# Attention in a mixture-of-experts layer: one 2048 wide exponential per key tile, and the last PV and Z matmuls of a pair issued ahead of the next pair's scores

## The reference

```python
def _L0_attn_ref(x, Wq, Wk, Wv):          # x: (4, 4096, 1024), 16 heads of 64
    q = (x @ Wq.T).reshape(N, S, H, hd).transpose(0, 2, 1, 3)
    k = (x @ Wk.T).reshape(N, S, H, hd).transpose(0, 2, 1, 3)
    v = (x @ Wv.T).reshape(N, S, H, hd).transpose(0, 2, 1, 3)
    energy = jnp.einsum('nhqd,nhkd->nhqk', q, k)
    attn = jax.nn.softmax(energy / jnp.sqrt(jnp.float32(hd)), axis=3)
    out = jnp.einsum('nhql,nhld->nhqd', attn, v)
    return out.transpose(0, 2, 1, 3).reshape(N, S, D)

def _L0_ffn_ref(tokens, router_w, router_b, expert_w):
...
    probs = jax.nn.softmax(logits, axis=-1)
    top_p, top_i = jax.lax.top_k(probs, TOP_K)
...
    for e in range(E):
        out = out + x @ expert_w[e] * gate[:, e:e + 1]
...
x = _layernorm(x + _L0_attn_ref(x, L0_attn_Wq, L0_attn_Wk, L0_attn_Wv), axis=-1)
x = _layernorm(x + _L0_ffn_ref(x, L0_ffn_router_w, L0_ffn_router_b, L0_ffn_expert_w), axis=-1)
```

## Time and profile before

| | us |
|---|---|
| median of 2 runs | 2903.71 (2902.87 to 2904.54) |
| the profiled execution, its time | 2902.06 |
| its span on the slowest core | 2900.5 (all cores: 2887.2 to 2900.5) |
| PE busy | 2337.3 (81% of the span) |
| ACT busy | 1113.9 (38%) |
| DVE busy | 719.2 (25%) |

### The profile page before, as it was taken

One profiled execution on the slowest core, in us unless ns is written; L12 is line 12 of the kernel. 1 busy time (PEld: TensorE's weight loads), 2 busy tenths in 40 slices (PEclk: granted clock), 3 DMA queues, 4 the chain that ended last, 5 costly groups with the idle time before them and its releaser, 6 DMA issues.

```text
span 2900.5 us, 31993 instructions; the slowest of 8 cores (2887.2 to 2900.5 us)
## 1 busy us (share of the span) xinstructions
PE 2337.3 (81%) x12032; PEld 896.7 (31%) x12032; DVE 719.2 (25%) x1555; ACT 1113.9 (38%) x1153; POOL 59.7 (2%) x80
## 2 busy tenths in 40 slices
PE   6996998898888888888886343999994434899995
PEld 2442322222222222222222111444441111344442
DVE  2332200000000000000002443333336344233336
ACT  0000288888888888888884100000000010000000
POOL 1000100000000000000000000000000000000000
PEclk9998999999999999999998666999997666999998
DMA  6755799950000000000002001122213000222121
GB/s 89 99 76 87 88 111 112 112 74 1 1 1 1 1 1 1 1 1 1 1 1 80 22 15 49 68 74 72 87 59 137 15 22 0 87 87 81 65 87 58
DMA packets 48017, 146.90 MB, mean 51 GB/s; under 512 B 2752, under 2 KB 23264, under 8 KB 46848
## 3 DMA queue, kind: packets, MB, share of 16 engines
q0 software_dynamic: 43264, 128.09, 24.0%
q1 hardware_dynamic: 4608, 16.78, 1.6%
HBM read 197.32 MB, written 41.94 MB: 82 GB/s over the span
## 4 chain that ended last, share of the span: by engine, by line
PE 62%; ACT 14%; DVE 10%; issue 9%; DMA 4%; DVEq 1%; ACTq 0%; POOL 0%; SPq 0%; POOLq 0%
PE s_PS L703 31%; PE s_PS L389 10%; ACT s_RC L450 9%; PE s_PS L288 6%; PE s_PS L225 5%; PE s_PS L301 4%; PE s_PS L246 4%; ACT s_RC L447 3%; DMA s_RC<-xfm 2%; DVE s_RC L526 2%; PE s_PS L313 1%; DMA s_RC<-xqf 1%; DMA s_RB<-ewb 1%; DVE s_RA L717 1%; DVE s_QO L363 1%
## 5 line engine op out<-in xcount | busy, mean ns | idle before, releaser
L703 PE MATMUL s_PS<-s_RB,s_QO 128*128 128x512 bf16 x4096 | 931.8, 391 | 137.2 <-DVE s_gates L659 67.4
L389 PE MATMUL s_PS<-s_QO,s_RA 64*128 64x512 bf16 x2048 | 571.8, 386 | 92.7 <-ACT s_RC L450 84.2
L447 ACT ACTIVATE s_RC<-s_PS,s_cb 128x1024 bf16<-128x1024 f32 x512 | 570.7, 1115 | 151.7 <-PE s_PS L389 151.7
L703 PEld LDWEIGHTS s_PS<-s_RB,s_QO 128*128 128x128 bf16 x4096 | 406.9, 100 | 658.0 <-issue 208.5
L450 ACT ACTIVATE s_RC<-s_PS,s_cb 128x1024 bf16<-128x1024 f32 x512 | 567.1, 1108 | 0.2 <-PE s_PS L389 0.2
L288 PE MATMUL s_PS<-s_RC,s_RB 128*64 128x512 bf16 x2048 | 329.6, 401 | 39.6 <-DVE s_RC L365 39.6
L761 ACT ACTIVATE s_tE<-s_tB 128x1 f32<-128x1 f32 x16 | 3.2, 203 | 880.6 <-DVE s_tB L753 880.6
L301 PE MATMUL s_PS<-s_RC,s_ozb 128*64 128x512 bf16 x2048 | 303.5, 380 | 0.9 <-ACT s_RC L450 0.9
L363 DVE CAST s_QO<-s_PS 128x1024 bf16<-128x1024 f32 x16 | 19.6, 1225 | 1106.6 <-PE s_PS L288 1106.6
L389 PEld LDWEIGHTS s_PS<-s_QO,s_RA 64*128 64x128 bf16 x2048 | 117.3, 94 | 508.2 <-issue 508.1
L720 DVE SCALAR_TENSOR_TENSOR s_RB<-s_PS,s_gates,s_RA 128x1024 f32<-128x1024 f32 x128 | 164.3, 1283 | 275.3 <-PE s_PS L703 275.3
(11 more groups left out here) (76 smaller groups left out, 643.5 us busy)
## 6 DMA issues: line engine op xcount, KB each, us to landing
s_RB<-ewb POOLq DMA_DIRECT2D x32, 2048.0 KB, 9.6
ewb<-ew POOLq DMA_DIRECT2D x16, 2048.0 KB, 169.1
s_RC<-xfm POOLq DMA_DIRECT2D x16, 1024.0 KB, 11.7
s_RC<-xtm SPq DMA_DIRECT2D x16, 512.0 KB, 3.6
y<-s_RC SPq DMA_DIRECT2D x16, 512.0 KB, 2.6
s_RC<-xqf POOLq DMA_DIRECT2D x4, 1024.0 KB, 18.0
s_RC<-wkT POOLq DMA_DIRECT2D x1, 2048.0 KB, 17.8
s_QO<-wvT POOLq DMA_DIRECT2D x1, 2048.0 KB, 27.0
```

The lines of the kernel that those rows point to most:

```text
L389: ins = t.matmul(PS[:, head * 1024 + qc * 512: head * 1024 + (qc + 1) * 512], RA[rows, c * SQ + kc * 128: c * SQ + (kc + 1) * 128], QO[row ...
L447: sc.activation(P[:, 0:1024], PS[:, 0:1024], AF.Exp, bias=cb3[:, :], scale=0.125).then_inc(sE, 1)
L703: ins = t.matmul(PS[:, pb + jh * 512: pb + (jh + 1) * 512], QO[:, dc * TOK + t_i * 128: dc * TOK + (t_i + 1) * 128], wbuf(par)[:, dc * 102 ...
```

## The change

The two exponentials of a step become one over all 2048 columns, which waits for all four score matmuls and raises sE once. The scores wait once, for the whole exponential of the step before, ahead of all four matmuls. The helpers `emit_zl` and `emit_pvl_fve` are gone: the last PV, the last three Z and DVE's two copies follow right behind the last step of the pair, PV first. `emit_ftz` stays behind the scores of step 2.

```diff
--- before.py
+++ after.py
@@ -331,43 +331,6 @@
         cvE.v += 1
         fvz_cnt[p_prev] = cvE.v
 
-    pvl_exp_need = {}
-
-    def emit_zl(p_prev):
-        cc = p_prev % NPAIR
-
-        def ftZl(t, cc=cc, exp_need=pvl_exp_need[p_prev]):
-            t.wait_ge(sE, exp_need)
-            for kcp in (NKT - 3, NKT - 2, NKT - 1):
-                ins = emit_z(t, cc, kcp, False, kcp == NKT - 1)
-            ins.then_inc(tV, 1)
-        q("tensor", ftZl)
-        ctV.v += 1
-        for kcp in (NKT - 3, NKT - 2, NKT - 1):
-            z_cnt[(p_prev, kcp)] = ctV.v
-
-    def emit_pvl_fve(p_prev):
-        cc = p_prev % NPAIR
-
-        def ftPVl(t, cc=cc, exp_need=pvl_exp_need[p_prev]):
-            t.wait_ge(sE, exp_need)
-            emit_pv(t, cc, NKT - 1, False, True).then_inc(tV, 1)
-        q("tensor", ftPVl)
-        ctV.v += 1
-        pv_cnt[(p_prev, NKT - 1)] = ctV.v
-        pvz_done = ctV.v
-        qc0p = (p_prev // NPAIR) * 1024
-
-        def fve(v, cc=cc, qc0=qc0p, pvz_done=pvz_done):
-            v.wait_ge(tV, pvz_done)
-            v.tensor_copy(QO[:, cc * TOK + qc0: cc * TOK + qc0 + 1024],
-                          PS[:, 2048:3072])
-            ins = v.tensor_copy(zs[:, :], PS[:, 3072:4096])
-            ins.then_inc(vE, 1)
-        q("vector", fve)
-        cvE.v += 1
-        fve_cnt[p_prev] = cvE.v
-
     for h in range(2):
         for c in range(NPAIR):
             p = h * NPAIR + c
@@ -382,8 +345,8 @@
                     if fw > 0:
                         t.wait_ge(vE, fw)
                         t.wait_ge(gC, consts_done)
+                    t.wait_ge(sE, exp_need)
                     for head in range(2):
-                        t.wait_ge(sE, max(0, exp_need - 1 + head))
                         rows = slice(head * 64, (head + 1) * 64)
                         for qc in range(2):
                             ins = t.matmul(
@@ -400,13 +363,8 @@
                 ctS.v += 2
                 s_done = ctS.v
 
-                if p > 0:
-                    if kc == 0:
-                        emit_zl(p - 1)
-                    elif kc == 1:
-                        emit_pvl_fve(p - 1)
-                    elif kc == 2:
-                        emit_ftz(p - 1)
+                if kc == 2 and p > 0:
+                    emit_ftz(p - 1)
 
                 if kc > 0:
                     kcp = kc - 1
@@ -443,19 +401,39 @@
                     if pv_need > 0:
                         sc.wait_ge(tV, pv_need)
                     P = pbuf(kc % 4)
-                    sc.wait_ge(tS, s_done - 1)
-                    sc.activation(P[:, 0:1024], PS[:, 0:1024], AF.Exp,
-                                  bias=cb3[:, :], scale=0.125).then_inc(sE, 1)
                     sc.wait_ge(tS, s_done)
-                    sc.activation(P[:, 1024:2048], PS[:, 1024:2048], AF.Exp,
+                    sc.activation(P[:, 0:2048], PS[:, 0:2048], AF.Exp,
                                   bias=cb3[:, :], scale=0.125).then_inc(sE, 1)
                 q("scalar", fse)
-                csE.v += 2
-
-            pvl_exp_need[p] = csE.v
-
-    emit_zl(2 * NPAIR - 1)
-    emit_pvl_fve(2 * NPAIR - 1)
+                csE.v += 1
+
+            def ftPVl(t, c=c, exp_need=csE.v):
+                t.wait_ge(sE, exp_need)
+                emit_pv(t, c, NKT - 1, False, True).then_inc(tV, 1)
+            q("tensor", ftPVl)
+            ctV.v += 1
+            pv_cnt[(p, NKT - 1)] = ctV.v
+
+            def ftZl(t, c=c):
+                for kcp in (NKT - 3, NKT - 2, NKT - 1):
+                    ins = emit_z(t, c, kcp, False, kcp == NKT - 1)
+                ins.then_inc(tV, 1)
+            q("tensor", ftZl)
+            ctV.v += 1
+            for kcp in (NKT - 3, NKT - 2, NKT - 1):
+                z_cnt[(p, kcp)] = ctV.v
+            pvz_done = ctV.v
+
+            def fve(v, c=c, qc0=qc0, pvz_done=pvz_done):
+                v.wait_ge(tV, pvz_done)
+                v.tensor_copy(QO[:, c * TOK + qc0: c * TOK + qc0 + 1024],
+                              PS[:, 2048:3072])
+                ins = v.tensor_copy(zs[:, :], PS[:, 3072:4096])
+                ins.then_inc(vE, 1)
+            q("vector", fve)
+            cvE.v += 1
+            fve_cnt[p] = cvE.v
+
     emit_ftz(2 * NPAIR - 1)
 
     p2_ve = cvE.v
```

## The result

The changed kernel is slower: 1.1006 of the time before, 95% interval 1.0991 to 1.102. The forecast was 3224 us and slower, range 3183 to 3400. The median of its 11 runs is 3241.66 us (3192.54 to 3328.88), that of before 2903.34. Some executions in any set have one half of the chip at a lower clock and are longer; the ratios leave them out, and so 1.1006 times the 2902 us of before, about 3194 us, is the figure to hold against the working.

The account below looks back on a forecast made before the run. It took ACT and PE, waiting for each other in a ring, to bound the attention stage. Steps 1479.7, passages 46.5 and start 6 made 1532.2 against 1212.2 us, +320.0, so 3224 us; range 3183 to 3400.

Parts of the forecast that it names:

- The chain: Attention steps: scores and exponential never overlap, so every link is paid; 2.89 us a step against 2.235, 1479.7 us in all.
- The slope from L623: Wide exponential: 0.80 ns per element, from L623's 307 ns for 16 elements to L447's 1115 ns, giving 1.94 us.
- The cover: Inside a step: PV and Z, 0.45 + 0.60 us, lie hidden under the exponential of 1.95 us.
- The passage: Between pairs of the attention stage: 3.1 us each, 15 times, 46.5 us; bounds 28 and 65 us.
- scores held back: At a passage: next pair's first scores queue behind PV and twelve Z, starting 1.87 us later than before.
- two slow scores: At a passage: PE idles over 2 us, the clock falls, four scores take 1.04 us, 0.38 more, in two steps.
- the push: At a passage: the transposes of L313 with PV push scores 3 back by 0.45 us.
- The start: First pair of the stage: the clock may take longer to rise; 6 us taken, between 0 and 11.
- The sum: Whole attention stage: 1479.7 + 46.5 + 6 = 1532.2 us against 1212.2, so +320.0 us.
- The clock: PE's clock in the stage: 0.95 or more expected inside a pair, although PE is busy only 60%.
- the likeliest case: The forecast's own case, about 3224 us with the clock kept up inside pairs; chance 0.74.
- this rival: Clock falls in the stage: mostly low, about 3407 us, chance 0.10; partly low, 3260 to 3400 us, chance 0.12.

Follow-up runs that it names:

- e3: Kernel before with both 1024 exponentials kept, but all four score matmuls wait for the second one; ratio 1.1183 to before, lowest 3240.2 us.
- e7: Changed kernel with the four score matmuls of each step issued twice; 3407.6 us at the lowest.
- e6: Changed kernel with the Z matmuls of each step issued twice; 3201.0 us at the lowest.
- e1: Kernel before with one 2048 wide exponential and one wait, passage between pairs left as before; ratio 1.1001 to before, lowest 3186.7 us.
- e2: Changed kernel with the two exponentials and their waits put back, leaving only the new passage order; lowest 2911.4 us against 2898.9 for the kernel before.
- e5: Changed kernel without the Z matmuls of steps 4 to 31; 3405.9 us, a single run.
- e4: Kernel before with Z put between the score matmuls of head 0 and head 1 from step 4 on; ratio 1.0062 to before.
- e8: Kernel before with a step's two halves taken by queries instead of heads; ratio 0.964 to before, lowest 2797.7 us.
- e11: e8 plus Z between the two score halves from step 4 on and the change's passage order; no ratio, lowest 2779.6 us against 2901.1 before.

## Why the prediction was right

- *The chain.* "The two never overlap, so a step is a closed chain, and every link is paid": shown by e3 and e7. Expected 2.89 us a step, measured 2.84. The links: 0.15 (said 0.14), scores 0.61 (0.685 said, from 0.66 and 0.71; the term most off, 0.075 x 512 = 38 us), 0.11, exponential 1.967 (1.95 said, 9 us the other way). The 0.66 is from a passage and the 0.71 from the start of the stage; inside a pair four scores in a row take 0.61. The slope from L623, 0.80 ns an element, was a little low: from 1115 to 1967 ns it is 0.83. The Trainium skill, "ScalarE: Activation LUTs", section What ACT_TABLE_LOAD costs, states 0.833 ns per element, and the trace agrees, (1967 - 1115) / 1024 = 0.832; its 1.99 us for the whole instruction is 0.02 over the measured one.
- *The cover.* PV and Z cost nothing under the exponential: shown by e6, where twice the Z matmuls leave the step at 2.84.
- *The passage.* 3.1 us said, 3.1 measured as the mean of fifteen, 3.34 at the one shown, with the same parts: scores held back (1.87), no stall for DVE, two slow scores, and transposes that push step 3. The exact agreement is part luck: the push, said to be 0.45 us, varies, and the passages lie between 2.5 and 3.34. What the order as such is worth the sum does not say, since it never priced the old order with one exponential: by e1 the new order is 2 us slower in the stage, and by e2, with two exponentials, 12 us.
- *The start.* 6 us said. The clock rose after three steps of 3.26 us, which is 1.3 us.
- *The sum.* +320 said, +289.8 in the stage. Steps account for 26 of the 30 us too many (0.05 x 512), the start for 5, the passages for nothing (46.5 said, 46.4 measured); the 1 left is within the rounding of the step (0.005 x 512).
- *The clock.* It held, as the likeliest case had it, and at the lower level a step is 3.26 us (3.24 said). e5 shows that the 0.22 given to this rival was not idle: without Z it falls. The Trainium skill, "TensorE: Matmul & The Clock Gate", section A second HAM failure mode: psum-queue depth-cycling, warns that short idle times between groups of matmuls can make the clock swing between its levels. The changed kernel has such an idle time of 1.24 us in every step and did not follow it (1.00 inside a pair); e5 came nearer to it, mostly at the lower level (0.54).

## What to carry to other kernels

One wide instruction in place of two saves a fixed cost, here 0.25 us of 2.22 by the durations and 0.10 us of a step by e3, but where two engines share a buffer by halves the halves are the double buffering (one half is filled while the other is read); merging them turns a step from about the longer of two engines' times into a chain of both, hand-overs included. Before widening an instruction, ask who could start on the first half. And choose the halves by what runs side by side on the producer: the same scores split by queries instead of heads gave 3.6%.

## What the runs showed of the hardware

- Taking matmuls away made the changed kernel 212 us slower by way of the clock (e5, 0.54), and a PE without a gap stayed at 0.50 for over 100 us (e4, 350 to 466), while in the changed kernel, busy 56% of the time by the windows view, it stood at 1.00. The busy share that a profile prints does not tell which level is granted.
- Two 64-row matmuls of 512 columns on the same half of the array hold PE 0.52 us, on both halves 0.33 us (e8), at the upper clock.
- Exponentials of 1024 that follow without a wait start 1.01 us apart, though each is 1.11 long; in e11, where ACT does not wait inside a pair, they start 1.00 apart (0.99 in the rows below) and the recorded duration grows to 1.17 here, so the duration is not the pace:

```profile
838.29 1.17 ACT L421 ACTIVATE s_RC<-s_PS,s_cb 128x1024 bf16<-128x1024 f32 x1
839.28 1.17 ACT L424 ACTIVATE s_RC<-s_PS,s_cb 128x1024 bf16<-128x1024 f32 x1
```
